# A 17-tap convolution split by node parity: three half-length products in place of four, on one Trainium2 core

## The reference, cut to what matters

```
xn     = layernorm(x)
h      = relu(bn1(conv1 @ xn))                 # 1x1 convolution, 128 -> 128 features
h      = bn2(conv1d(h, conv2_w, pad=8))        # 17 taps along the node axis, 128x128 each
x_conv = relu(h + xn)
A      = exp(-dist(s, s)) * adj                # s: 3-dim embedding of xn; 1024 x 1024
x_nmp  = A @ relu(msg(xn))
x1     = x + GRU([x_conv, x_nmp], xn)
out    = x1 + (x2 + ffn(x2) * w on 511 nodes by rank of w = x2 @ wr),  x2 = layernorm(x1)
```

## Time and profile before

| | |
|---|---|
| median of 3 runs | 687.42 us (686.48 to 688.18) |
| the profiled execution: its own time / its span | 689.14 us / 687.3 us |
| mean granted TensorE clock (share of full) | 0.966 |
| PE busy | 623.5 us, 91% of the span, 2880 matmuls |
| DVE busy | 485.7 us, 71% |
| ACT busy | 311.6 us, 45% |
| POOL busy | 159.7 us, 23% |

### The profile page before, as it was taken

One profiled execution on the slowest core, in us unless ns is written; L12 is line 12 of the kernel. 1 busy time (PEld: TensorE's weight loads), 2 busy tenths in 40 slices (PEclk: granted clock), 3 DMA queues, 4 the chain that ended last, 5 costly groups with the idle time before them and its releaser, 6 DMA issues.

```text
span 687.3 us, 8513 instructions
## 1 busy us (share of the span) xinstructions
PE 623.5 (91%) x2880; PEld 465.9 (68%) x2880; DVE 485.7 (71%) x1241; ACT 311.6 (45%) x501; POOL 159.7 (23%) x137
## 2 busy tenths in 40 slices
PE   2999999999999999999999999999999996687280
PEld 2776787678767876787678767876787664455160
DVE  4735376778877887778787878787876786878240
ACT  3624562456244624462446244624462434456150
POOL 2000002000430043004400440034005101277745
PEclk9999999999999999999999999999999998799785
DMA  6440600260026002600260016001600150013201
GB/s 218 160 146 5 240 1 1 63 243 1 12 81 246 0 14 81 245 1 13 80 245 1 8 54 245 1 8 55 245 1 24 39 185 1 8 48 97 77 18 34
DMA packets 35835, 55.82 MB, mean 81 GB/s; under 512 B 4167, under 2 KB 25427, under 8 KB 35536
## 3 DMA queue, kind: packets, MB, share of 16 engines
q1 hardware_dynamic: 29776, 48.87, 20.2%
q0 software_dynamic: 6016, 6.40, 3.0%
HBM read 44.68 MB, written 14.74 MB: 86 GB/s over the span
## 4 chain that ended last, share of the span: by engine, by line
PE 83%; DVE 6%; DMA 4%; issue 3%; POOL 2%; ACT 2%; SPq 0%; POOLq 0%; DVEq 0%; ACTq 0%
PE N L1078 16%; PE C L978 11%; PE C L979 11%; PE C L980 11%; PE M L1058 8%; PE D L1054 4%; PE M L978 2%; PE M L979 2%; PE M L980 2%; DMA adjb<-in_conv_w 2%; PE N L978 1%; PE D L980 1%; PE D L979 1%; PE D L978 1%; PE N L979 1%
## 5 line engine op out<-in xcount | busy, mean ns | idle before, releaser
L515 ACT ACTIVATE tr<-D 128x512 f32<-128x512 f32 x128 | 76.4, 597 | 171.0 <-PE D L1054 171.0
L978 PE MATMUL C<-hH,wc 128*128 128x512 f32 x272 | 110.1, 405 | 0.0
L979 PE MATMUL C<-hL,wc 128*128 128x512 f32 x272 | 107.2, 394 | 0.0
L980 PE MATMUL C<-hH,wc 128*128 128x512 f32 x272 | 107.0, 394 | 0.0
L371 POOL TENSOR_TENSOR rstd<-ve,vec 128x8 f32<-128x8 f32 x8 | 13.3, 1658 | 341.1 <-DVE ve L652 341.1
L1054 PE MATMUL D<-V,U 128*128 128x512 f32 x128 | 88.8, 694 | 0.0
L1058 PEld LDWEIGHTS M<-cst,adjb 128*128 128x128 f32 x512 | 63.3, 140 | 37.0 <-issue 18.9
L1058 PE MATMUL M<-cst,adjb 128*128 128x128 f32 x512 | 76.8, 272 | 0.0
L789 DVE TENSOR_TENSOR tz<-tr,M 128x512 f32<-128x512 f32 x64 | 43.7, 683 | 38.9 <-ACT tr L515 38.5
L407 POOL DMA_INDIRECT sel<-R,ridx x64 | 65.1, 1017 | 18.8 <-issue 18.2
L1078 PE MATMUL N<-tz,msgF 128*128 128x512 f32 x128 | 64.2, 593 | 0.0
(11 more groups left out here) (212 smaller groups left out, 1255.2 us busy)
## 6 DMA issues: line engine op xcount, KB each, us to landing
adjb<-in_adj SPq DMA_DIRECT2D x8, 4096.0 KB, 13.6
adjb<-sel SPq DMA_DIRECT2D x8, 516.0 KB, 5.2
out<-R SPq DMA_DIRECT2D x8, 512.0 KB, 3.5
xall<-in_x SPq DMA_DIRECT2D x7, 512.0 KB, 5.0
adjb<-in_weights SPq DMA_DIRECT2D x1, 1280.0 KB, 8.9
adjb<-in_conv_w SPq DMA_DIRECT2D x1, 1088.0 KB, 11.1
sel<-R,ridx POOLq DMA_INDIRECT x64, 2.3
xall<-in_x SPq DMA_DIRECT2D x2, 256.0 KB, 3.1
```

The lines of the kernel that those rows point to most:

```text
L515: nc.scalar.activation(E[:, u % NE, :], Db[u % NH][:, :], ACT.Exp, scale=-1.0).then_inc(exp_ok, 1)
L978: MM(out_, wgt(0), hi, start=start, stop=False)
L979: MM(out_, wgt(0), lo, start=False, stop=False)
L980: return MM(out_, wgt(1), hi, start=False, stop=stop)
```

## The change

With a and b the nodes of even and odd number (512 each), E the sum over the 9 even taps and O over the 8 odd taps, the even outputs are E a + O b, the odd ones E b + O a', where a' is a moved by one place: four half-length products. The change computes three, from a common part G = (E + O) b: the even outputs are G + E(a - b), the odd ones G + O(a' - b). In matmuls of 128x512 that is 9 x 3 for G (`conv_common`; eight sums of an even and an odd tap, one even tap alone), 9 x 3 for E (`conv_even`) and 8 x 3 for O (`conv_odd`): 78 in place of 102 a batch.

- The sums of taps are made once at the start: `raw_s` is a DVE addition of 128x1024 numbers, and `PIECES` has a fourth piece (split by ACT and DVE as the others) that lies ahead of the last in both queues.
- `relu_conv1` writes the two parities (`hab`) and the high part of b (`bH`); DVE makes `bL` (`lo_of_b`), now behind `new_gate`.
- POOL makes the differences a - b and a' - b (`differences`, 128x512 and 128x513), ACT their high parts (`hi_of_differences`), DVE the low ones (`lo_of_differences`).
- ACT brings G to SBUF with scale and shift (`common_part`); POOL adds the layer's input to it for each parity (`residual`, two of 128x512), behind `inv_std(b + 1)` in its queue. DVE adds E's and O's banks to that (`conv_sum`, in place of ACT's `bn2` and DVE's `conv_pre`), the second behind `weigh(2)`; `weigh(0)` waits for POOL's residual.
- `EARLY` is at taps 3, 5 and 7 of `conv_odd`; `state_back` stands behind the fourth tap of `conv_even`.

```diff
-EARLY = {11: 0, 13: 1, 15: 2}
+SPLIT = 4
+EARLY = {3: 0, 5: 1, 7: 2}
...
+            def differences(b):
+                wait(pool, ab_ok, b, NH, NH)
+                if b > 1:
+                    pool.wait_ge(rank_ok, T * (b - 2) + T - 3)
+                a, bb = hab[:, 0, :], hab[:, 1, :]
+                nc.gpsimd.tensor_tensor(eF, a[:, PH:PH + HALF], bb[:, PH:PH + HALF],
+                                        ALU.subtract).then_inc(ef_ok, 1)
+                nc.gpsimd.tensor_tensor(fF, a[:, PH:PH + HALF + 1], bb[:, PH - 1:PH + HALF],
+                                        ALU.subtract).then_inc(ef_ok, 1)
+            def residual(b, q):
+                wait(pool, g1_ok, b, 1, 1)
+                wait(pool, sL_ok, b, NH, NH)
+                for k in range(2):
+                    nc.gpsimd.tensor_tensor(wk[:, half(k)], G1, parity(xT[:, q, :], k), ALU.add).then_inc(pre_ok, 1)
...
+            def common_part(b):
+                wait(act, g1_ps, b, 1, 1)
+                wait(act, e_ok, b - 1, NH, 1)
+                nc.scalar.activation(G1, C0[:, :], ACT.Identity, bias=col(V_SH2), scale=col(V_SC2)).then_inc(g1_ok, 1)
...
+            def conv_sum(b, k):
+                wait(dve, c2_ps, b, 2, k + 1)
+                wait(dve, pre_ok, b, 2, k + 1)
+                hs = half(k)
+                STT(wk[:, hs], (C1, C0)[k][:, :], col(V_SC2), wk[:, hs], ALU.mult, ALU.add).then_inc(y2_ok, 1)
...
+            TT(raw_s, raw_c2[:, 0:KO * D], raw_c2[:, KE * D:], ALU.add).then_inc(sum_w, 1)
...
-                conv2(b, 0)
+                conv_common(b)
+                conv_even(b, range(0, SPLIT))
                 if not first:
                     state_back(b - 1, Nb)
-                conv2(b, 1)
+                conv_even(b, range(SPLIT, KE))
+                conv_odd(b)
```

More of the change, by code:

```diff
@@ L31 @@
 K2 = 17
+KO = K2 // 2
+KE = KO + 1
 PAD = K2 // 2
+PH = PAD // 2
+LP = HALF + PAD
 HID = 4 * D
@@ L717, in lo_of_xT, with lo_of_b, lo_of_differences @@
                        ALU.subtract).then_inc(xTL_ok, 1)
[L719 to L724 removed]
+            def lo_of_b(b):
+                wait(dve, ab_ok, b, NH, NH)
+                wait(dve, bH_ok, b, NH, NH)
+                at = slice(PH, PH + HALF)
+                TT(bL[:, at], hab[:, 1, at], f32(bH[:, at]), ALU.subtract).then_inc(bL_ok, 1)
+            def lo_of_differences(b):
+                wait(dve, efH_ok, b, 2, 1)
+                TT(ef[:, 2, PH:PH + HALF], eF, f32(ef[:, 0, PH:PH + HALF]), ALU.subtract).then_inc(efL_ok, 1)
+                wait(dve, efH_ok, b, 2, 2)
+                TT(ef[:, 3, PH - 1:PH + HALF], fF, f32(ef[:, 1, PH - 1:PH + HALF]), ALU.subtract).then_inc(efL_ok, 1)
             def new_gate(b, h):
@@ L1013, in messages, with conv_taps, conv_common, conv_even @@
                     i.then_inc(m_ps, 1)
-            def conv2(b, h):
-                if isinstance(b, int) and b == 0:
-                    pe.wait_ge(wL_ok, 2)
-                wait(pe, hL_ok, b, NH, NH)
-                if h == 0:
-                    wait(pe, tz_ok, b - 1, NH, 2)
-                for k in range(K2):
-                    if h == 1 and k in EARLY:
+            def conv_taps(bank_, at, hi, lo, ks, start, stop):
+                for k in ks:
+                    cols = slice(k, k + HALF)
+                    w = at if k < KO else KO
+                    i = three(bank_, lambda v: wc2[:, v, (w + k) * D:(w + k + 1) * D], hi[:, cols], lo[:, cols],
+                              start and k == ks[0], stop and k == ks[-1])
+                return i
+            def conv_common(b):
+                if b == 0:
+                    pe.wait_ge(wL_ok, 3)
+                wait(pe, bL_ok, b, 1, 1)
+                wait(pe, tz_ok, b - 1, NH, 2)
+                conv_taps(C0[:, :], 0, bH, bL, range(KE), True, True).then_inc(g1_ps, 1)
+            def conv_even(b, ks):
+                wait(pe, efL_ok, b, 2, 1)
+                i = conv_taps(C1[:, :], KO, ef[:, 0, :], ef[:, 2, :], ks, ks[0] == 0, ks[-1] == KO)
+                if ks[-1] == KO:
+                    i.then_inc(c2_ps, 1)
+            def conv_odd(b):
+                wait(pe, g1_ok, b, 1, 1)
+                wait(pe, efL_ok, b, 2, 2)
+                for k in range(KO):
+                    if k in EARLY:
                         front(b, EARLY[k])
-                    a = slice(h * HALF + k, h * HALF + k + HALF)
-                    i = three(Cb[h][:, :], lambda w: wc2[:, w, k * D:(k + 1) * D], hH[:, a], hL[:, a], k == 0, k == K2 - 1)
+                    i = conv_taps(C0[:, :], KO + KE, ef[:, 1, :], ef[:, 3, :], (k,), k == 0, k == KO - 1)
                 i.then_inc(c2_ps, 1)
@@ L1098, in gru @@
                     wait(pe, W_ok, b - 1, NH, NH)
-                wait(pe, xcL_ok, b, NH, h + 1)
+                wait(pe, xcL_ok, b, 2, 2)
                 three(r[:, :], wh(0), *X, True, False)
```

146 lines of the change are left out of this document (80 added, 66 removed).

## The result

The changed kernel takes 700.07 us (698.42 to 701.36, 4 runs) against 687.14 (686.48 to 688.18) before; the ratio is 1.0185, 95% interval 1.0158 to 1.0213. The profiled execution took 698.42 (span 696.5) against 689.14 (687.3). I had said 689, 679 to 697.

The account below looks back on a forecast made before the run. PE was taken as the bound, but only just covering DVE's work ahead of `weigh(0)`. Middle batches +11.0, batch 1 -3.8, batch 7 -5.1, batch 0 -0.6 gave +1.5 us: forecast 689 us, range 679 to 697.

Parts of the forecast that it names:

- What bounds the kernel: Middle batches: PE is the bound, but with fewer matmuls it waits for `weigh(0)` at the third `front`'s transposes; gain 0.1 us.
- (a): Start of a middle batch: U comes 0.35 us earlier through shorter `relu_conv1` and POOL differences; -0.35 us.
- (b): `normalise` ahead of the first `weigh`: POOL's two residual additions hold DVE up; +1.6 us a middle batch, between 0.5 and 2.2.
- (c): Behind PE's gap at the third `front`: the clock falls to half, delaying the first product; +1.05 us, between 0 and 1.7.
- DVE stands still while POOL's addition runs: Read where L397 runs: L824 takes 1.14 us beside it and 0.23 without; a 128x512 product 2.30 in place of 0.69.
- From there on the units are PE's again: Middle batches from the first product with the messages on: PE sets the pace; no further loss was priced.
- batch 0: First `front` waits for the adj load, landing at 41.6 against 42.08; with one tap less behind it, -0.6 us.
- Batches 1 and 7: Batch 1 has no ranks, batch 7 no `normalise`, so PE's saving mostly counts: -3.8 and -5.1 us.
- slower: Rival: both residual additions hold DVE in full and the clock stays low longer; 3.45 us a middle batch, 695 us; chance 0.24.
- The full gain: Rival: PE stays the bound and all 44.7 us of the removed matmuls come, 643 us; chance 0.04.

Follow-up runs that it names:

- e9: The changed kernel as it stands, repeated on another chip: 702.64 us, 1.006 of the kernel before.
- e14: The changed kernel with POOL's `base_rows` put off until DVE's second rank step behind the weighs: 696.30 us, 1.013 of the kernel before.
- e16: Changed kernel, next batch's statistics and `normalise` among late weighs, `base_rows` and indirect DMAs later (DMAs unmoved in last batch), batch 0's adjacency load earlier: 649.57 us, 0.946.
- e4: Changed kernel with next batch's statistics and `normalise` moved among weighs 10 to 15, POOL's power behind `base_rows`: 664.76 us, 0.953 of the kernel before.
- e11: Changed kernel, next batch's statistics and `normalise` among late weighs, `base_rows` and indirect DMAs later in all batches, batch 0's adjacency load earlier: 655.73 us, 0.954.
- e3: The changed kernel with POOL's `base_rows` made as eight additions of 128x128 in place of one: 704.25 us, 1.011 of the kernel before.
- e1: The changed kernel with POOL's residual put ahead of the power that `normalise` waits for: 696.29 us, 0.999 of the kernel before.
- e6: The changed kernel with `base_rows` put off until DVE's second rank step behind the weighs, on another chip: 699.29 us, 1.001 of the kernel before.

## Why the prediction was wrong, by its steps

*What bounds the kernel* was right: the first `front` at t = 21.0 as reckoned, the wait at the third's transposes, ended by `weigh(0)`, nothing gained by the matmuls alone.

*(a) U's time* was -0.35 and is -0.04 (t = 11.93 against 11.97). POOL's 128x512 takes 1.27 us, not half of 2.2, and the second difference 1.73 beside `bL`, whose end it seems to have waited for; that case was priced, the durations weren't.

*(b) The held `normalise`*, +1.6, is 1.96 in DVE's row, inside its bounds of 0.5 to 2.2. Of it 0.46 are given back ahead of `weigh(1)`, where DVE had waited 0.94 for POOL's second power (first line below, of the kernel before) and waits 0.48 now. That leaves 1.50, near the 1.6, but by another route: I had the first addition in full and half of the second, and both held DVE in full, one instruction each. In batch 5 the first two of the eight took 1.33 and 1.31 us, and over the run L714 has the second line (ns min/median/max): POOL's second addition stepped in between two back-to-back instructions of DVE.

```profile
390.84 0.66 DVE L806 TENSOR_SCALAR R<-xall,mean,rstd 128x128 f32<-128x128 f32 x2 [0.94 <-POOL rstd L376]
...
L714 DVE TENSOR_SCALAR xn<-xall,mean,rstd x64: 331/336/1342, 8.0 to 466.4; 128x128 f32<-128x128 f32 x64
```

By the Trainium skill (SBUF — State Buffer, Who interferes with whom) whoever of the two issues first has the shared pair of ports for its whole instruction, and the other is blocked. For the single instruction the trace agrees: the first addition starts at 389.96 and takes 1.29 us, the first of the eight starts at 390.01 and takes 1.33 in place of 0.34.

The sentence "DVE stands still while POOL's addition runs" is too wide, though. What L397 held were instructions such as L824 and L815; before the change L821 (1.21 us) ran beside it in its usual time. In e9 a `weigh` (L847, one operand in PSUM) ran wholly beside `base_rows` in its usual 0.69 us, and L873 behind it was held.

*(c) The clock*, +1.05, is +1.24 up to the first product, in size and place as forecast. But the prediction let it be back by then ("if it is low for as long here"), and in batches 4 and 6 it was low for 10.2 us in place of 6.8 and cost another 1.1 and 1.3 behind the first product. In the mean of the five batches (c) is 1.7, the end of its bounds. Why the same gap brings one or the other isn't shown.

By (a), (b) and (c) as forecast the first product should come at 35.0 and comes at 35.5, a miss of half a microsecond a batch: 0.3 of it from (a), 0.2 from (c).

*The step that failed* is "From there on the units are PE's again". They are only while DVE keeps up and the clock is back, and behind the first product the batches lose another 0 to 2.1 us, 6.3 in all: 3.9 in PE's waits for late weighs (d), for which the prediction had no term, and 2.4 in the longer low clock. I had the very row, a product held 2.30 us by L397 in batch 7, and used it as a measure for (b), not as an event that a shift of DVE against POOL could bring into every batch. Before, `base_rows` fell on the end of `node_weights`, where DVE's delay of 0.9 us made no wait of PE. The first `weigh` now comes 2.0 us later and the second 1.5, `base_rows` only 1.3 (t = 42.85 against 41.6) in batches 3 to 6, and it meets a DVE instruction ahead of the next `weigh` whole (`products` in 3 and 5, `conv_lo` in 4 and 6). `weigh(8)` or `weigh(7)` then comes 1.9 to 2.4 us late, and PE waits at one or two sets of transposes, 0.9 to 1.1 us in sum. In batch 2 `base_rows` came 1.2 us later for its DMAs and cost nothing, by luck of the place. e14 moves it and takes these waits away.

The sum: the forecast's +1.5, plus five times 1.67 (0.8 of (d), 0.5 of the clock behind the first product and 0.5 by which that came late, less 0.1 behind the last), less 0.6 in batch 0 (-0.6 forecast, -1.2 measured, of which -1.45 is the earlier landing and so chance) is +9.2. Batches 1 and 7 were right to 0.2 us. The rival "slower" at 695 had the sign and two of the three causes: both additions in full, and a low clock that lasts longer, if in two batches of five. Its 3.45 us a middle batch are near the 3.87 measured, but it had a larger (b) and nothing for (d). The range was short since every end of it came from (b) and (c); no case stood for a collision that didn't exist before. The full gain, 0.04, was rightly low for this kernel, and e16 shows what stood in its way: the order of DVE's work, nothing in the arithmetic.

## What to carry to other kernels

When matmuls are taken from an engine that only just covers another's work, list what the other does ahead of the first point where they meet, and move that first; e4 turned a loss into 0.95 without a change in the arithmetic. Work moved to GpSimd was paid for by VectorE wherever it met one of the instructions that it holds: place it where VectorE's lateness hides (here beside the ranks, 0.3 us, or behind the weighs), and after any shift ask which VectorE instruction every old GpSimd addition now falls on. A loss that differs from batch to batch asks for the clock of each batch before a cause is named: the same gap brought 6.8 us of low clock in three batches and 10.2 in two. And work that is off the path in the early batches can still delay the last one (the indirect DMAs of e11).

## What the runs showed of the hardware that I hadn't expected

GpSimd's addition of two float32 operands takes 1.27 us for 128x512, 2.21 for 128x1024 and 3.61 for eight of 128x128, so small ones are dear. GpSimd's short additions in a row held one VectorE instruction through six of them (2.91 us, e3), while GpSimd did step in between VectorE's eight. TensorE's clock, which falls within the gap, was low for 6.8 us in three batches and for 10.2 in two, with gaps of 6.62 to 6.66 us in all five. And the runs differ by chip in more than speed: on that of e1 to e4 and that of e6 to e9 the other engines started up to 2.4 us behind PE's matmuls at one place of most batches, and the kernel before was 1.4 to 1.6% slower there (whether by this no trace of it shows), so that the change's loss read 0.6% in e9 in place of 1.85%.
